# Layer 3's full attention: three PSUM banks for the scores of its first pass, two for the ring of its second

## The chip, the cores and the metric

One core of a Trainium2 chip runs the whole program. The metric is the device time of one execution in microseconds (us): less is better. Five engines work side by side, each on its own queue of instructions in a fixed order: TensorE (PE: matmuls and, apart from them, the loads of their weights, PEld), VectorE (DVE), ScalarE (ACT), GpSimd (POOL) and SyncE (SP, which issues DMAs). They wait for one another through semaphores. Matmuls write to PSUM, which is cut into eight banks of 512 fp32 columns on 128 partitions, and VectorE and ScalarE read them from there.

## What is computed

The program is a chain of fourteen sublayers on a tensor x of 4 sequences of 512 tokens of 128 features: four "layers", each a half-weighted block, an attention and the half-weighted block again. The change concerns layer 3's attention alone, on the sum of everything before it:

```
q = (x @ Wq.T + bq).reshape(b, l, H, HD).transpose(0, 2, 1, 3)      # H = 16 heads of HD = 8
k, v = the same with Wk, bk and Wv, bv
q, k = _apply_rope(q, cos, sin), _apply_rope(k, cos, sin)
scores = jnp.einsum('bhsd,bhed->bhse', q, k) / np.sqrt(HD)          # every token with every token: 512 x 512
attn = jax.nn.softmax(scores, axis=-1)
out = jnp.einsum('bhse,bhed->bhsd', attn, v)
x = x + out.transpose(0, 2, 1, 3).reshape(b, l, e) @ Wo.T + bo
```

No mask is applied, so each of the 16 heads of each of the 4 sequences has a full 512 x 512 table of scores. On either side of it stand the two halves of layer 3's other block (`l3_layer`), which is local attention over windows of 64 tokens and a gated feed-forward.

## The kernel before

**Slots.** The program is a list of units, one for each sublayer and sequence, and slot k does three things side by side: the core of unit k, the preparation ("pre") of unit k + 1 and the closing work ("post") of unit k - 1. The steps of these streams are merged on every engine in an order that is written out by hand for each slot (`ORDERS`, strings such as `a4b1c2`: four steps of stream a, one of b, two of c). An engine goes from one slot to the next without a barrier. The change keeps all of these strings as they are, so every engine's instructions keep their order. Full attention has four slots, one for each sequence; below they are called passes 0 to 3. Pre and post work that runs beside the core is called side work here. In pass 0 it is the post of a layer-3 block (L663, L388, the gated feed-forward at L2502 to L2536) and the pre of the next attention (L388, L439, the turns at L586 with their copies at L595); in passes 1 and 2 the post of the attention before (L688, L715, L720) and again the pre of the next; in pass 3 the pre of a layer-3 block (L2199, L2206, L2242 to L2304).

**The core of the attention, `attend8`.** It serves three kinds of attention (FULL, CAUSAL, BLOCK32). It works through the heads in four groups of four and computes every score twice.

- First pass: `score(i)`, L1151, i = 0 to 63, multiplies one tile of 128 queries with all 512 keys into a bank of `SCORES`. VectorE takes the negated row maximum of it (L1251). With NS banks, score i may start only when the maximum of score i - NS is done (the wait in `score`).
- GpSimd splits a group's maxima into three bf16 parts and writes them beside the queries (L1261, L1267), TensorE turns the queries with them (`turn_q`, L1170, two pairs for each group) and ScalarE copies them back (L1277).
- Second pass: `shifted_score(i)`, L1187, i = 0 to 63, computes the scores transposed, keys by queries, with the maximum already subtracted, into a bank of the ring `RING`; ScalarE takes the exponential of it (L1300) into one of eight buffers. The turned queries of `turn_q` go through the same ring. With NR banks, entry n of the ring may be written only when ScalarE is done with entry n - NR.
- `weigh`, L1210: after every four shifted scores, eight instructions multiply the probabilities of four heads and one tile of keys with the values into the bank `OUT`; ScalarE copies the result of a group (L1283). It weighs what was issued at least three units before.

In TensorE's order the first `LEAD` = 22 first-pass scores stand alone, with side work between them. Then come a turn and, for i = 0 to 41, a shifted score and a first-pass score by turns (score 22 + i beside shifted score i); for i = 42 to 63 there are only shifted scores. Four units and a `weigh` are called a quad below, quads 0 to 15. `half_rows` gives even and odd heads different halves of the array's rows, so two neighbouring matmuls of either pass can run at the same time if nothing holds the second one.

**Banks.** Of the eight, attend8 has six (`SCORES`, `RING` and `OUT`); 6 and 7 are those of the pre and of the post work.

Of the kernel before, what the change touches and what calls it, by code (L numbers as in the profile page):

```python
# [1065 lines left out]
FULL, CAUSAL, BLOCK32 = range(3)  # L1066


def attend8(nc, m, note, a, kind, before):
# [23 lines left out]
    weighed = [max(r for r, unit in enumerate(second) if unit[0][1] in kts or kind == BLOCK32) for kts in kinds]  # L1093
    NW = len(weighed)
    LEAD = N1 + 6
    SCORES, RING, OUT = (0, 1), (2, 3, 4), 5
    NS, NR = len(SCORES), len(RING)
    TURN_AT = max(N2 - 3, 0)
    PROBS = 8
# [460 lines left out]
def l1_ffn_core(nc, m, note, a, b, l, before):  # L1560
    return attend8(nc, m, note, a, CAUSAL, before)
# [544 lines left out]
def l2_attn_core(nc, m, note, a, b, l, before):  # L2106
    return attend8(nc, m, note, a, BLOCK32, before)
# [16 lines left out]
def l3_attn_core(nc, m, note, a, b, l, before):  # L2124
    return attend8(nc, m, note, a, FULL, before)
# [1318 lines left out]
```

## Times and profile before

| | us |
|---|---|
| median of 3 runs | 2942.89 |
| lowest and highest | 2940.99, 2950.08 |
| the profiled execution | 2941.67 |
| its span, first to last instruction | 2939.9 |
| TensorE, VectorE, ScalarE busy over the span | 2544.9, 2167.9, 1664.1 |
| from the first score of pass 0 to the last weighing of pass 3 | 323.6 |

The page of the profile gives busy time and the costliest groups over the whole span; the four passes of full attention are 11% of it, so they are read from windows. "PEclk" there is the clock that TensorE was granted, as a share of 2.4 GHz; 0.5 is 1.2 GHz. A busy TensorE is not TensorE at its peak: the time of a matmul includes the drain of its pipeline.

### The profile page before, as it was taken

How to read it: one execution, taken by the hardware profiler on the slowest of the kernel's cores; microseconds unless marked ns; L12 is line 12 of the kernel's file. 1: busy time of each engine (PE TensorE's matmuls, PEld its weight loads, DVE VectorE, ACT ScalarE, POOL GpSimd, SP SyncE). 2: the span in 40 equal slices, each digit the busy share in tenths (PEclk: the TensorE clock that was granted, in tenths of full speed). 3: DMA queues.
4: the chain of work that ended last, by engine and by line, in shares of the span. 5: the costliest groups of instructions: out<-in, count | busy, mean ns of one | idle time of the engine just before them, and what ended most of it. 6: DMA issues, size and time to landing. Idle time of an engine off the chain costs nothing.

```text
span 2939.9 us, 63499 instructions
## 1 busy us (share of the span) xinstructions
PE 2544.9 (87%) x24589; PEld 1617.3 (55%) x24589; DVE 2167.9 (74%) x5133; ACT 1664.1 (57%) x4036; POOL 787.8 (27%) x810
## 2 busy tenths in 40 slices
PE   6878889788898888988877988999988889989998
PEld 3556666554455544547755875565653222556655
DVE  4856557778887668877567567888877777888883
ACT  2334443466642367753476546767747666676773
POOL 1010001111111111121332246546511114455650
PEclk9879998899999999999999999999989998999999
DMA  3623420000000000014600661010100000001001
GB/s 114 243 41 57 81 62 1 1 1 1 1 1 1 1 1 1 1 58 168 252 6 1 216 217 30 15 28 17 28 3 3 1 1 13 16 16 28 18 19 28
DMA packets 123078, 131.95 MB, mean 45 GB/s; under 512 B 81941, under 2 KB 101653, under 8 KB 121242
## 3 DMA queue, kind: packets, MB, share of 16 engines
q1 hardware_dynamic: 120250, 122.70, 14.0%
q8 instruction: 196, 3.21, 0.5%
q0 software_dynamic: 2048, 4.20, 0.4%
q10 hardware_dynamic: 480, 0.98, 0.1%
q14 instruction: 104, 0.85, 0.1%
HBM read 80.73 MB, written 29.04 MB: 37 GB/s over the span
## 4 chain that ended last, share of the span: by engine, by line
PE 45%; DVE 27%; ACT 10%; issue 7%; POOL 5%; DMA 2%; SPq 0%; DVEq 0%; POOLq 0%; ACTq 0%
DVE nm L1251 6%; PE ps L1210 4%; PE ps L586 3%; PE ps L1990 3%; PE ps L1187 3%; PE ps L2199 3%; PE ps L1151 3%; PE ps L2365 2%; ACT hand L550 2%; PE ps L663 2%; PE ps L439 2%; DVE pre L2285 2%; PE ps L2502 2%; POOL ss L2276 1%; PE ps L265 1%
## 5 line engine op out<-in xcount | busy, mean ns | idle before, releaser
L1251 DVE TENSOR_REDUCE nm<-ps 128x2 f32<-128x256 f32 (+2 forms) x704 | 424.0, 636 | 65.3 <-PE ps L1151 42.4
L1300 ACT ACTIVATE core<-ps 128x512 f32<-128x512 f32 x672 | 358.7, 591 | 93.0 <-PE ps L1192 48.4
L380 POOL TENSOR_TENSOR rstd<-ve,weights 128x4 f32<-128x4 f32 x80 | 83.0, 1038 | 879.5 <-DVE ve L357 828.1
L2271 POOL TENSOR_TENSOR pre<-pre,sin 128x512 f32<-128x512 f32 x128 | 231.2, 1825 | 226.9 <-ACT pre L2242 200.1
L1151 PE MATMUL ps<-hand 128*128 128x128 bf16 (+4 forms) x1024 | 246.0, 314 | 44.9 <-DVE nm L1251 39.8
L550 ACT COPY hand<-ps 64x512 bf16<-64x512 bf16 x336 | 194.7, 579 | 132.1 <-PE ps L586 81.7
L1187 PE MATMUL ps<-hand 128*128 128x128 bf16 (+4 forms) x1024 | 225.3, 307 | 21.7 <-ACT hand L550 15.1
L2405 ACT ACTIVATE core<-ps,nm 128x128 f32<-128x128 f32 x512 | 181.9, 379 | 67.0 <-DVE nm L2422 66.0
L2276 POOL TENSOR_TENSOR ss<-ss,weights 128x16 f32<-128x16 f32 x64 | 196.6, 3072 | 71.6 <-DVE ss L2291 69.9
L2199 PE MATMUL ps<-weights,pre 128*128 128x512 f32 x384 | 200.0, 624 | 11.2 <-ACT hand L2253 6.6
L1261 POOL CAST hand<-nm 128x16 bf16<-128x16 f32 x192 | 59.0, 308 | 492.6 <-DVE nm L1251 484.3
L1210 PE MATMUL ps<-core,hand 128*32 128x512 f32 (+3 forms) x2048 | 179.4, 445 | 8.3 <-ACT otok L1283 5.6
L265 PE MATMUL ps<-identb 128*128 128x256 bf16 x1052 | 165.6, 286 | 16.9 <-PEq L3046 14.3
L1187 PEld LDWEIGHTS ps<-hand 128*128 128x128 bf16 (+1 forms) x1024 | 81.6, 98 | 179.1 <-ACT core L1300 94.9
L1151 PEld LDWEIGHTS ps<-hand 128*128 128x128 bf16 (+1 forms) x1024 | 86.1, 98 | 162.9 <-DVE nm L1251 112.4
L2365 PE MATMUL ps<-hand 64*64 64x128 f32 (+1 forms) x2048 | 136.2, 273 | 0.0
L2365 PEld LDWEIGHTS ps<-hand 64*64 64x64 f32 x2048 | 104.7, 135 | 44.4 <-issue 44.4
L265 PEld LDWEIGHTS ps<-identb 128*128 128x128 bf16 x1052 | 100.3, 102 | 50.5 <-issue 35.1
L586 PE MATMUL ps<-identb,hand 128*128 128x128 bf16 x768 | 79.4, 229 | 55.4 <-DVE pre L502 17.4
L2502 PE MATMUL ps<-post,weights 128*128 128x512 f32 (+1 forms) x192 | 105.6, 632 | 22.3 <-DVE post L2530 13.8
L2422 DVE TENSOR_REDUCE nm<-ps 128x4 f32<-128x512 f32 x128 | 87.2, 682 | 44.3 <-PE ps L2365 43.9
L2285 DVE TENSOR_TENSOR pre<-pre,cos 128x1024 f32<-128x1024 f32 x64 | 108.0, 1688 | 13.9 <-ACT pre L2242 13.8
(352 smaller groups left out, 6313.6 us busy)
## 6 DMA issues: line engine op xcount, KB each, us to landing
hand<-in_experts SPq DMA_DIRECT2D x48, 836.0 KB, 4.7
shear<-post SPq DMA_DIRECT2D x64, 256.0 KB
core<-in_experts SPq DMA_DIRECT2D x12, 836.0 KB, 5.1
core<-shear SPq DMA_DIRECT2D x128, 64.0 KB, 2.2
hand<-hand SPq DMA_DIRECT2D x16, 512.0 KB, 4.4
hand<-hand SPq DMA_DIRECT2D x16, 384.0 KB, 5.6
core<-in_stream SPq DMA_DIRECT2D x2, 2048.0 KB, 7.7
shear<-pre SPq DMA_DIRECT2D x16, 256.0 KB
```

What stands on the lines that cost most here:

```text
L265: nc.tensor.matmul(out, m.identb, m.identb.unsqueeze(1).to_broadcast([P, FILL // P, P]), start=True, stop=True)
L550: ins = copy(a.QX[64 * e:64 * e + 64, q_slot(2 * pair + e), :], src[64 * e:64 * e + 64, :])
L1151: ins = nc.tensor.matmul(b[:, n * nk:(n + 1) * nk], q[:, qt * P:(qt + 1) * P], k[:, lo:lo + nk], start=kind != BLOCK32 and n == 0, stop=Tr ...
L1187: ins = nc.tensor.matmul(b[:, n * w:(n + 1) * w], k[:, kt * P:(kt + 1) * P], q[:, s:z], start=kind != BLOCK32 and n == 0, stop=True, skip_ ...
L1210: ins = nc.tensor.matmul(m.ps[32 * j:32 * j + 32, OUT, s:z], a.V[:, kt, 9 * h:9 * h + 32], prob8[:, i % PROBS, n * w:(n + 1) * w], start=( ...
L1251: nc.vector.tensor_reduce(nm_of(unit), src, AX.X, ALU.max, negate=True).then_inc(negmax, 1)
L1300: nc.scalar.activation(prob8[:, i % PROBS, 0:w], m.ps[:, RING[at % NR], 0:w], ACT.Exp).then_inc(ring_out, 1)
L2199: nc.tensor.matmul(banks[at % N], s.hT[:, t * P:(t + 1) * P], qkv[:, l, i, :], start=True, stop=True).then_inc(lane.filled, 1)
L2271: ins = nc.gpsimd.tensor_tensor(o[:, :, :, z:z + hl], x[:, :, :, y0:y0 + hl], sn[:, t, :, z:z + hl].unsqueeze(2).to_broadcast([P, 2, LH, h ...
L2276: nc.gpsimd.tensor_tensor(m.ss[:, 1, 0:2 * LH], m.ss[:, 0, 0:2 * LH], m.weight["half"][:, 0:2 * LH], ALU.pow).then_inc(rooted, 1)
L2365: ins = nc.tensor.matmul(out[rows, r * P + at:(r + 1) * P], a.Q3[rows, c, n * WIN:(n + 1) * WIN], a.K3[rows, c, lo:(n + 1) * WIN], start=F ...
L2405: nc.scalar.activation(prob[:, i % NP3, r * P:(r + 1) * P], bank(m, S[i % 2])[:, r * P:(r + 1) * P], ACT.Exp, bias=m.nm[:, 4 * i + r:4 * i ...
```

## The change

One line. For full attention the six banks are dealt out anew; the two other kinds keep theirs. Nothing else of the program changes, and no instruction is added, removed or moved.

```diff
     LEAD = N1 + 6
-    SCORES, RING, OUT = (0, 1), (2, 3, 4), 5
+    SCORES, RING, OUT = ((0, 1, 2), (3, 4), 5) if kind == FULL else ((0, 1), (2, 3, 4), 5)
     NS, NR = len(SCORES), len(RING)
```

NS becomes 3: score i waits for the maximum of score i - 3, not i - 2. NR becomes 2: a ring entry waits until ScalarE is done with the entry two before it, not three.

## Rows read from the trace of the kernel before

**Rows 1.** Instruction groups of the four passes: count, busy, mean ns, idle before and releaser.

```profile
L1251 DVE TENSOR_REDUCE nm<-ps 128x1 f32<-128x512 f32 x256 | 164.2, 684 | 36.6 <-PE ps L1151 34.0
L1300 ACT ACTIVATE core<-ps 128x512 f32<-128x512 f32 x256 | 140.4, 614 | 30.4 <-PE ps L1187 29.8
L1151 PE MATMUL ps<-hand 64*128 64x512 bf16 x256 | 88.4, 424 | 25.0 <-DVE nm L1251 23.6 <-ACT core L1300 0.4
L1187 PE MATMUL ps<-hand 64*128 64x512 bf16 x256 | 72.1, 391 | 3.1 <-ACT core L1300 2.0 <-ACT hand L1277 0.5
```

**Rows 2.** Busy time by stretch: stretch, length, each engine, clock, DMA share, GB/s.

```profile
2202.90:2247.10 44.20, 40.24 (x236) 12.14 (x235) 38.59 (x75) 37.66 (x76) 8.66 (x17) 1.00 0.02 4
...
2267.10:2287.20 20.10, 16.14 (x52) 5.31 (x49) 14.51 (x24) 3.50 (x11) 1.25 (x5) 0.66 0.00 1
2287.20:2325.10 37.90, 33.46 (x224) 11.01 (x224) 35.51 (x64) 29.55 (x60) 6.10 (x14) 1.00 0.00 1
2325.10:2343.10 18.00, 16.22 (x128) 5.84 (x126) 6.09 (x19) 15.07 (x28) 2.27 (x6) 1.00 0.00 1
...
2362.10:2400.30 38.20, 32.97 (x225) 10.70 (x225) 35.04 (x60) 30.06 (x60) 6.00 (x13) 1.00 0.00 1
...
2439.60:2480.20 40.60, 39.54 (x220) 13.05 (x219) 36.98 (x60) 32.75 (x64) 17.72 (x17) 1.00 0.00 1
```

**Rows 3.** Timeline, first 22 scores of pass 1: start, length, instruction, [idle before].

```profile
2271.32 0.58 PE L1151 MATMUL ps<-hand 64*128 64x512 bf16 x1 [0.21 <-DVE nm L1251]
...
2271.83 1.12 PE L388 MATMUL ps<-weights,pre 128*128 128x128 f32 x4
...
2276.20 1.65 PE L439 MATMUL ps<-weights,pre 128*128 128x384 f32 x2
```

**Rows 4.** The same stretch, VectorE's maxima.

```profile
2267.58 5.05 DVE L1251 TENSOR_REDUCE nm<-ps 128x1 f32<-128x512 f32 x8 [1.85 <-PE ps L1151]
...
2273.53 3.48 DVE L1251 TENSOR_REDUCE nm<-ps 128x1 f32<-128x512 f32 x5 [0.89 <-PE ps L1151]
...
2278.75 3.48 DVE L1251 TENSOR_REDUCE nm<-ps 128x1 f32<-128x512 f32 x5 [1.74 <-PE ps L1151]
...
2283.97 1.29 DVE L1251 TENSOR_REDUCE nm<-ps 128x1 f32<-128x512 f32 x2 [1.74 <-PE ps L1151]
```

**Rows 5.** Timeline, quad 5 of pass 1, which has both passes' scores.

```profile
2307.60 0.39 PE L1187 MATMUL ps<-hand 64*128 64x512 bf16 x2
...
2308.02 2.06 ACT L1300 ACTIVATE core<-ps 128x512 f32<-128x512 f32 x4 [0.26 <-PE ps L1187]
...
2309.67 0.37 PE L1151 MATMUL ps<-hand 64*128 64x512 bf16 x1 [0.30 <-DVE nm L1251]
```

**Rows 6.** Timeline, quad 14 of pass 1, which has shifted scores alone.

```profile
2338.64 0.60 PE L1187 MATMUL ps<-hand 64*128 64x512 bf16 x3
...
2339.07 2.06 ACT L1300 ACTIVATE core<-ps 128x512 f32<-128x512 f32 x4 [0.32 <-PE ps L1187]
...
2339.72 0.39 PE L1187 MATMUL ps<-hand 64*128 64x512 bf16 x1 [0.47 <-ACT core L1300]
...
2340.03 1.07 PE L1210 MATMUL ps<-core,hand 128*32 128x512 f32 x8
```

**Rows 7.** Timeline, quads 12 and 13 of pass 1.

```profile
2334.27 1.03 ACT L595 COPY hand<-ps 128x1024 bf16<-128x1024 bf16 x1
...
2334.51 0.39 PE L1187 MATMUL ps<-hand 64*128 64x512 bf16 x2
...
2335.17 2.59 ACT L1300 ACTIVATE core<-ps 128x512 f32<-128x512 f32 x5
...
2335.86 0.88 PE L1187 MATMUL ps<-hand 64*128 64x512 bf16 x2
```

**Rows 8.** Timeline, ScalarE in quad 8 of pass 0.

```profile
2240.84 1.28 ACT L1300 ACT_TABLE_LOAD   x1
2242.13 1.08 ACT L1300 ACTIVATE core<-ps 128x512 f32<-128x512 f32 x2
```

**Rows 9.** The same quad, TensorE.

```profile
2240.26 0.40 PE L1187 MATMUL ps<-hand 64*128 64x512 bf16 x2
...
2242.79 0.39 PE L1187 MATMUL ps<-hand 64*128 64x512 bf16 x1 [0.38 <-ACT core L1300]
```

## Prediction, made before the changed kernel ran

> **What bounds the kernel now.** I read the groups of the four passes first, then the busy times by stretch, then timelines. The groups show the case for the change: before first-pass scores TensorE stood idle 23.6 us for VectorE's maxima, before shifted scores 2.0 us for ScalarE's exponentials [rows 1]. That is 25.6 us of 323.6, and it is the wrong sum to build on, since an idle time says nothing of what would come next. The stretches show three regimes in each pass [rows 2], for which pass 1 stands: a **lead** of 20.1 us (the first 22 scores; ScalarE busy 3.50, the clock at 0.66), a **middle** of 37.9 us (both kinds of scores; VectorE busy 35.51, 94%) and a **tail** of 18.0 us (shifted scores alone; VectorE busy 6.09, TensorE 16.22, ScalarE 15.07). The third score bank can act in the lead and the middle. The third ring bank is used in the middle and the tail. So gain and loss lie in different places and each is costed there.
>
> **The lead.** A lone score and its maximum hold a bank for about 0.39 + 0.68 us plus two handovers. In the lead the first eight maxima take 5.05 us, later ones 3.48 us for five, that is 0.70 each, where TensorE runs at the low clock (a matmul of 0.58 and more) and two banks can't keep VectorE fed [rows 3, 4]. With three banks VectorE's own pace holds, (5.05 - 0.68)/7 = 0.62 us. Some 14 of the 22 scores go by 0.70, so 14 x 0.08 = 1.1 us. The larger part is side work: while TensorE does L388, or L439 and what follows it, VectorE runs dry and waits 0.89, 1.74 and 1.74 us [rows 3, 4]. A third bank lets TensorE begin each block one maximum earlier, 0.62 to 0.70 us, and each wait shrinks by that: 3 x 0.65 = 2.0. The 1.85 us before the first maximum remain: no score existed. Together 3.1 us; laid out score by score with these durations (block at L388 from 2271.83 to about 2270.94, L439 from 2276.20 to 2274.3, the turn about 3.0 us earlier) it is 3.0. The order of GpSimd, which splits the maxima of 16 scores ahead of the turn, doesn't move, and it has 3 us to spare in pass 1. The other leads have the same three or so blocks, some shorter; I take 2.7 us on average: **-11 us** for four, between -7 (pauses only, passes 2 and 3 weaker) and -14.
>
> **The middle.** Upper bound of the gain: VectorE's idle time in the four middles, 5.6 + 2.4 + 3.2 + 3.6 = 14.8 us (length less busy) [rows 2]. It won't all come, for the ring holds the same queue. In quad 5 two shifted scores start at 2307.60, the exponentials at 2308.02 with a pitch of (2.06 - 0.60)/3 = 0.49, and the last first-pass score at 2309.67 [rows 5]. With two ring banks the third shifted score waits for the first exponential, 2308.02 + 0.60 + 0.06 = 2308.68, the fourth for the second, 2309.17, and the last first-pass score, no longer waiting for a maximum, starts 0.22 later, at 2309.39: 0.28 us earlier than now. ScalarE is the faster of the two readers (0.49 against 0.60), so where it has nothing else to do the trade is a small gain; but VectorE can't follow in a middle where it has 6% to spare. I take -1.2 us in passes 1 and 2 each and nothing in pass 3. Where ScalarE has other work in its order, the price is the other way: in quad 8 of pass 0 a table load holds the exponentials until 2242.13, and the second of the two shifted scores of 2240.26 would have to wait for the first of them, 2242.13 + 0.60 + 0.06 = 2242.79, instead of running at once [rows 8, 9]. Queued behind it on TensorE are a score, two side blocks (1.6 us) and the shifted score that now waits for the same exponential until 2242.79; so of the 2.5 us about 2 are lost. Less common, smaller cases are in the same pass. Pass 0: +2. **Middle: 0 us**, between -14 (all of VectorE's idle time) and +8 (2 us of such stalls in every pass).
>
> **The tail.** Here nothing is gained: no first-pass scores are left, and the three-deep ring is what hides ScalarE. Quad 14: three shifted scores start at 2338.64 together, the fourth at 2339.72 when the first exponential is done, the weighing at 2340.03 [rows 6]. With two, the third starts at 2339.07 + 0.60 + 0.05 = 2339.72, the fourth one exponential later, 2340.21, the weighing at 2340.53: +0.49 us, on TensorE, which has no other idle time there to give. ScalarE's own work moves by only 0.1, since its queue was full; but TensorE weighs (1.0 us) between the quads in any case, and the ring is too shallow to hide that. Quads 11 and 14 cost 0.49 each; a block of side work between the pairs (0.55 us of turns) doesn't help, as the fourth waits for the second exponential still. Quads 12 and 13 hold copies of ScalarE's: the second shifted score of 2334.51 must wait for the exponential that starts at 2335.17, after the copy of 1.03 us, that is until 2335.83, +1.3; the next ones, which now wait themselves (0.88 us for two), give back 0.4, and quad 13 adds its 0.49: +1.44 for both [rows 7]. Quad 10 has a turn whose entries fill both banks: +0.5 to +0.9; quad 9 +0.2. Pass 1: 0.2 + 0.9 + 0.49 + 1.44 + 0.49 = 3.5. The same count is 3.6 in pass 0, 3.7 in pass 2, and about 4 in pass 3, where a clock of 0.5 in part of the tail stretches it. **Tail: +15 us**, between +8 (0.49 in four quads of each pass and nothing else) and +20.
>
> **Sum.** -11 + 0 + 15 = +4 us. The profiled execution took 2941.67 us (its span is 2939.9, 1.8 us lie around it) and is 1.2 us below the median of the three runs. From the median: 2942.9 + 4 = 2947; from the profiled one 2945.7. I forecast **2946 us**.
>
> **The rivals.**
> *The third score bank wins.* TensorE leaves each middle early and VectorE's idle time goes: -12 in the leads, -12 in the middles, +13 in the tails: -11, so 2932 us. For it speaks that VectorE's reductions are the slower reader (684 against 614 ns, x256 each) and that 34.0 us of its idle time are put down to L1151 [rows 1]. Against it: some 7 us of these are waits for the first score of a pass, four like the 1.85 us of pass 1 [rows 4], and in the middle the waits of the ring sit in the same order.
> *The short ring starves TensorE behind ScalarE's other work* (the case on the other side). The place is every shifted score whose predecessor but one stands behind a copy or a table load on ScalarE; the price is that instruction's length, 1.03 or 1.28 us, once per occurrence, with side work queued behind it [rows 7, 8]. It decides as soon as such stalls aren't covered by VectorE's backlog in the middle: 2 us in each middle (+8) and 20 in the tails, less 11: +17, 2960 us. For it: ScalarE is busy 37.66 of 44.20 us in pass 0's middle [rows 2]. Against: in passes 1 and 2 VectorE is behind then, and hides them.
> *The clock.* The lead shows what spaced-out scores do: TensorE was paced by the maxima, one score every 0.60 us, and its clock fell to 0.66 on average, 1.2 GHz for two thirds of the stretch, while the tail ran at 1.00 [rows 2, 4]. If the tail, with half a microsecond more idle in each quad, falls too for a third of its 16.2 us of work, this third takes twice as long: +5 less the waits it covers, about +3 a pass, +12 on top: 2958 us. The Trainium skill ("TensorE: Matmul & The Clock Gate", A second HAM failure mode: psum-queue depth-cycling) speaks against this change: a TensorE that cycles through a queue of PSUM banks with short idles between groups can lose and regain its full clock over and over. By that rule the time would be this rival's; the trace doesn't bear it out so far, as quad 14, with 0.47 us idle in 2.39, ran at full clock.
> *It does nothing that can be seen*, the bank indices being a relabelling where neither wait binds: 2943 us. The waits of [rows 1] speak against it.
>
> **How the numbers follow.** The forecast's case has 0.50, the third bank's 0.20, the starved ring's 0.18, the clock's 0.08, no effect 0.04. A measurement of this kernel can tell about 0.3%, 8.8 us, from no change: 2934.1 to 2951.7. The forecast's own range is 2937 to 2955 (lead and tail each off by 4, the middle by 5), so 0.06 of its 0.50 are slower than that bound. Faster: 0.20. Same: 0.44 + 0.04 and a little of the two slow cases, 0.50. Slower: 0.30. The range of 8 in 10 reaches into both sides: 2931 to 2961.
>
> **What would show it.** Right: the stretch of the first 22 scores of pass 1 shrinks from 20.1 to about 17 us, its pauses before maxima from 1.74 to about 1.1; the idle time before L1151 put down to L1251 falls from 23.6 to under 14; that before L1187 put down to L1300 grows from 2.0 to 12 or more; quad 14 becomes 2.9 us long; tails of 18.0 become 21.5; the middles keep their length within a microsecond or two. Wrong: leads that shrink by less than 1.5 us, because something other than a bank holds TensorE there; tails that stay near 18 us; middles that shrink by more than 2 us each; a granted clock below 0.9 in the tails of passes 0 to 2. Everything outside the four passes should keep its length; if it doesn't, the sum misses a term.

## The result

The changed kernel takes 2959.61 us (median of seven executions; 2956.06 to 2963.8), the kernel before 2942.7 (2938.76 to 2950.08): 1.0058 times as long, with a 95% interval of 1.0044 to 1.0071, or 16.9 us slower. Forecast were 2946 us, 3 us slower; the range of 2931 to 2961 holds the result by 1.4 us at its upper end, and the narrower range of the forecast's own case, 2937 to 2955, does not hold it.

Where it went is read from the lengths of the three regimes, in each pass: the lead from the first first-pass score to the first shifted score, the middle from there to the start of the weighing that ends quad 9, the tail from there to the next pass (in pass 3 to where the weights of the last weighing are loaded, 0.9 us before its last matmul ends). Summed over the four passes, in us, from one profiled execution each (quad 9, whose 0.2 us a pass the forecast counted with the tail, lies in the middle here):

| | leads | middles | tails | all |
|---|---|---|---|---|
| before | 81.7 | 160.9 | 80.1 | 322.8 |
| changed | 71.4 | 171.2 | 94.7 | 337.3 |
| difference | -10.3 | +10.3 | +14.6 | +14.5 |
| forecast | -11 | 0 | +15 | +4 |

The profiled execution of the changed kernel took 2962.08 us, its span 2960.3, which is 20.4 more than before. Of that 14.5 lie in the passes and 6.3 ahead of them, where the two kernels are alike: pass 0 begins at 2188.08 and not at 2181.78. In the profiles of this study it begins between 2179.5 and 2188.1, and in the changed kernel with only the gelu behind that point altered at 2181.24, so this part is taken as the spread of an execution and no effect.

First the groups of the four passes of the changed kernel, which answer to [rows 1] (count, busy, mean ns, idle before and releaser):

```profile
L1251 DVE TENSOR_REDUCE nm<-ps 128x1 f32<-128x512 f32 x256 | 163.3, 682 | 37.6 <-PE ps L1151 37.1
L1300 ACT ACTIVATE core<-ps 128x512 f32<-128x512 f32 x256 | 143.4, 601 | 46.2 <-PE ps L1187 45.5
L1151 PE MATMUL ps<-hand 64*128 64x512 bf16 x256 | 82.8, 415 | 8.5 <-DVE nm L1251 8.4
L1187 PE MATMUL ps<-hand 64*128 64x512 bf16 x256 | 79.5, 394 | 27.3 <-ACT core L1300 19.3 <-ACT hand L1277 6.1
```

TensorE's idle time ahead of first-pass scores fell from 25.0 to 8.5 us, that ahead of shifted scores rose from 3.1 to 27.3: 16.5 us gone, 24.2 new. Of the 27.3, 6.1 end with L1277, the copy of turned queries, which had 0.5. Both readers stand idle longer than before (VectorE 37.6 against 36.6, ScalarE 46.2 against 30.4), though one of them has a bank more.

The stretches that answer to [rows 2], of the changed kernel (length, busy time of each engine, clock, DMA share, GB/s):

```profile
2206.20:2254.60 48.40, 42.64 (x238) 12.16 (x237) 39.09 (x76) 38.66 (x76) 8.67 (x17) 0.96 0.02 4
...
2277.20:2295.40 18.20, 15.91 (x51) 5.67 (x47) 13.97 (x24) 3.45 (x10) 1.26 (x5) 0.62 0.00 0
2295.40:2334.80 39.40, 33.07 (x229) 10.23 (x232) 35.93 (x64) 30.21 (x60) 6.12 (x14) 1.00 0.00 1
2334.80:2355.90 21.10, 16.90 (x129) 5.83 (x129) 5.90 (x18) 15.73 (x28) 2.27 (x6) 1.00 0.00 1
...
2373.70:2412.00 38.30, 33.33 (x225) 10.42 (x225) 35.20 (x60) 30.44 (x60) 5.92 (x13) 1.00 0.00 1
2412.00:2435.00 23.00, 16.93 (x118) 5.17 (x117) 5.82 (x19) 15.69 (x28) 2.27 (x6) 0.93 0.00 1
...
2452.40:2497.50 45.10, 40.92 (x224) 11.88 (x223) 38.35 (x61) 34.35 (x65) 18.04 (x17) 1.00 0.00 1
2497.50:2525.40 27.90, 21.44 (x109) 6.68 (x112) 11.62 (x26) 17.35 (x33) 10.31 (x9) 0.82 0.15 34
```

Middles: 44.2 became 48.4 (pass 0), 37.9 became 39.4, 38.2 became 38.3 and 40.6 became 45.1 (pass 3). Pass 1 stands for lead and tail: 20.1 became 18.2, 18.0 became 21.1. Next the maxima in the lead of pass 1, against [rows 4]:

```profile
2277.74 4.87 DVE L1251 TENSOR_REDUCE nm<-ps 128x1 f32<-128x512 f32 x8 [2.58 <-PE ps L1151]
2282.89 3.08 DVE L1251 TENSOR_REDUCE nm<-ps 128x1 f32<-128x512 f32 x5 [0.28 <-PE ps L1151]
2287.30 3.08 DVE L1251 TENSOR_REDUCE nm<-ps 128x1 f32<-128x512 f32 x5 [1.34 <-PE ps L1151]
2291.73 1.29 DVE L1251 TENSOR_REDUCE nm<-ps 128x1 f32<-128x512 f32 x2 [1.34 <-PE ps L1151]
```

Pauses of 0.89, 1.74 and 1.74 us became 0.28, 1.34 and 1.34, and five maxima take 3.08 and not 3.48 us, though the granted clock was no higher (0.62 in this lead, 0.66 before). Both parts of the forecast gain are there; the pauses gave 1.4 us of the 2.0 laid out, the pace 1.0 of 1.1, and 0.4 of that is lost again between the last maximum shown and the first shifted score.

Two quads of pass 1, TensorE's timeline in the changed kernel. First quad 5, against [rows 5], with its weighing at the end:

```profile
2316.24 0.39 PE L1187 MATMUL ps<-hand 64*128 64x512 bf16 x2
2316.47 0.38 PE L1151 MATMUL ps<-hand 64*128 64x512 bf16 x2
2317.32 0.39 PE L1187 MATMUL ps<-hand 64*128 64x512 bf16 x1 [0.47 <-ACT core L1300]
2317.55 0.38 PE L1151 MATMUL ps<-hand 64*128 64x512 bf16 x1
2317.81 0.39 PE L1187 MATMUL ps<-hand 64*128 64x512 bf16 x1
2318.03 0.38 PE L1151 MATMUL ps<-hand 64*128 64x512 bf16 x1
2318.34 0.64 PE L1210 MATMUL ps<-core,hand 128*32 128x512 f32 x4
```

Then quad 14, against [rows 6]:

```profile
2350.94 0.39 PE L1187 MATMUL ps<-hand 64*128 64x512 bf16 x2
2352.01 0.87 PE L1187 MATMUL ps<-hand 64*128 64x512 bf16 x2 [0.69 <-ACT core L1300]
2352.82 0.64 PE L1210 MATMUL ps<-core,hand 128*32 128x512 f32 x4
```

In quad 5 the third shifted score waits for the first exponential, the fourth comes 0.49 later, and nothing waits for a maximum: the last first-pass score starts 1.79 us after the first shifted one (2.07 before), and the quad, weighing to weighing, takes 3.09 us, not 3.38. In quad 14 two shifted scores start together where three did, and the quad takes 2.88 us, not 2.39. Both were laid out so in the prediction.

### The profile page after: what moved, and what is told of

The parts are those of the page before. It is cut to its first block, busy times and chain, and to the rows that moved or that the text cites. A ratio compares the mean times of both kernels' runs of the same rounds, so it can differ in the third digit from the quotient of the medians.

```text
span 2960.3 us, 63433 instructions
## 1 busy us (share of the span) xinstructions
PE 2549.8 (86%) x24519; PEld 1620.7 (55%) x24589; DVE 2167.6 (73%) x5133; ACT 1671.4 (56%) x4036; POOL 788.0 (27%) x810
## 4 chain that ended last, share of the span: by engine, by line
PE 45%; DVE 26%; ACT 10%; issue 7%; POOL 5%; DMA 2%; SPq 0%; another core or an unknown queue 0%; DVEq 0%; ACTq 0%; POOLq 0%
DVE nm L1251 5%; PE ps L1210 4%; PE ps L1187 3%; PE ps L586 3%; PE ps L1990 3%; PE ps L2199 3%; PE ps L2365 2%; PE ps L1151 2%; ACT hand L550 2%; PE ps L663 2%; PE ps L439 2%; PE ps L2502 2%; DVE y L1603 2%; DVE pre L2285 2%; POOL ss L2276 1%
## 5 line engine op out<-in xcount | busy, mean ns | idle before, releaser
L1187 PE MATMUL ps<-hand 128*128 128x128 bf16 (+4 forms) x1005 | 226.9, 308 | 42.8 <-ACT core L1300 22.3
L1151 PE MATMUL ps<-hand 128*128 128x128 bf16 (+4 forms) x997 | 232.1, 311 | 27.7 <-DVE nm L1251 24.3
L2276 POOL TENSOR_TENSOR ss<-ss,weights 128x16 f32<-128x16 f32 x64 | 196.7, 3074 | 71.9 <-DVE ss L2291 70.3
L265 PE MATMUL ps<-identb 128*128 128x256 bf16 x1052 | 164.3, 285 | 16.9 <-PEq L3046 14.2
L2365 PEld LDWEIGHTS ps<-hand 64*64 64x64 f32 x2048 | 104.1, 135 | 44.2 <-issue 44.2
```

Source lines behind the costliest of these rows:

```text
L265: nc.tensor.matmul(out, m.identb, m.identb.unsqueeze(1).to_broadcast([P, FILL // P, P]), start=True, stop=True)
L1151: ins = nc.tensor.matmul(b[:, n * nk:(n + 1) * nk], q[:, qt * P:(qt + 1) * P], k[:, lo:lo + nk], start=kind != BLOCK32 and n == 0, stop=Tr ...
L1187: ins = nc.tensor.matmul(b[:, n * w:(n + 1) * w], k[:, kt * P:(kt + 1) * P], q[:, s:z], start=kind != BLOCK32 and n == 0, stop=True, skip_ ...
L2276: nc.gpsimd.tensor_tensor(m.ss[:, 1, 0:2 * LH], m.ss[:, 0, 0:2 * LH], m.weight["half"][:, 0:2 * LH], ALU.pow).then_inc(rooted, 1)
L2365: ins = nc.tensor.matmul(out[rows, r * P + at:(r + 1) * P], a.Q3[rows, c, n * WIN:(n + 1) * WIN], a.K3[rows, c, lo:(n + 1) * WIN], start=F ...
```

## Experiments

Two theories were set against each other for the 10.3 us of the middles, which the forecast did not have. A: the ring of two costs there what it costs in the tail, above all where the turned queries fill it and where ScalarE has other work in front of an exponential. B: the third score bank lets TensorE run into side work that waits for VectorE. The other runs test lead and tail apart, and look for a deal of the banks that keeps the gain alone. For those where banks change with the phase, the round robin was replaced by a plan: for each score or ring entry, in TensorE's order, the bank of those allowed that was used longest ago, and a wait for that bank's last user.

**The short ring alone.**

```diff
-    SCORES, RING, OUT = (0, 1), (2, 3, 4), 5
+    SCORES, RING, OUT = ((0, 1), (2, 3), 5) if kind == FULL else ((0, 1), (2, 3, 4), 5)
```

> Full attention keeps two score banks and has a ring of two (one PSUM bank stands unused), so only the loss of the change is in it. Theory A (the short ring costs in the middle too: turned queries that fill both its entries, and shifted scores behind other work of ScalarE): leads unchanged within 0.5 us each, tails +3.7 us on average as in the changed kernel (+15), middles +10 or more over the four passes, since the third score bank isn't there to give anything back: 25 to 35 us slower than before. Theory B (the middle loses because TensorE, with three score banks, runs ahead into side work that waits for VectorE, and the ring has no part in it): middles +0 to +3, tails +15: 15 to 18 us slower.

Measured: 2968.83 us against 2940.7, ratio 1.0096 (1.0076 to 1.0116), 28 us slower. Leads 80.8, middles 173.9, tails 97.4: -0.9, +13.0 and +17.3. So the middles lose as much without the third score bank as with it, and a little more; theory B as the only cause falls. On balance the third score bank, which the changed kernel has beside the short ring, gives 2.7 us back in the middles. The tails are 2.7 us longer than in the changed kernel. The low clock has a part in that: the tail of pass 3 had a granted clock of 0.71 here, 0.82 in the changed kernel.

**The third score bank in the leads alone.** The first 22 scores go over banks 0, 1 and 2, then everything as before.

```diff
+    LEAD_SCORES, SCORES, RING, TAIL_RING, OUT = (((0, 1, 2), (0, 1), (2, 3, 4), (2, 3, 4), 5) if kind == FULL else ...
```

> Only the first 22 scores of each pass go over three banks (the third is a bank of the ring, which is empty then); from the first turn on two and three as before. If the four leads give what they gave in the changed kernel (-3.0, -2.0, -1.3, -4.1 us) and nothing is given back: 10 us faster than before, middles and tails unchanged within 1 us each. If VectorE's work only moves (it is the bound of the middles of passes 1 and 2), up to half comes back in the middles: 5 us faster.

Measured: 2935.59 us against 2940.7, ratio 0.9981 (0.9970 to 0.9992), 5.1 us faster. In its profile leads 70.3, middles 161.1, tails 80.1: -11.4 us in the leads and nothing given back. The profiled execution took 2929.91 us, the median is 5.7 us above it. So the profile shows the gain of the first expectation and the median half of it. The leads themselves move with the granted clock: with the same three banks, that of pass 0 takes 16.7 us here at 0.80 and 18.2 in the changed kernel at 0.62, that of pass 3 takes 19.3 here at 0.65 and 17.3 there at 0.90. How they fall out in the other executions isn't known, and this stays open. Every quad from quad 1 on is as before to within 0.02 us, so the plan of the banks in itself changes nothing.

**The changed kernel with its third ring bank back in the tail.** Score banks (0, 1, 2), ring (3, 4), and (2, 3, 4) once the last first-pass score is issued.

```diff
+    LEAD_SCORES, SCORES, RING, TAIL_RING, OUT = (((0, 1, 2), (0, 1, 2), (3, 4), (2, 3, 4), 5) if kind == FULL else ...
```

> The changed kernel, but once the last first-pass score of a pass is issued the ring has three banks again (the freed score bank joins it). Both theories: the tails return to their lengths before (about -15 us against the changed kernel), leads and middles stay those of the changed kernel: 0 to 2 us slower than before. If the tail's loss were not the ring's depth but what the middle leaves behind, it would stay 10 us slower or more.

Measured: 2944.42 us against 2940.7, ratio 1.0004 (0.9994 to 1.0015): no difference. Leads 70.4, middles 174.3, tails 77.8. The tails are back, 16.9 us below those of the changed kernel, quads 10 to 14 of passes 0 to 2 at the lengths of before to within 0.15 us. The tail's loss is the depth of the ring, and nothing that the middle leaves behind. The middle's loss stands (3.1 us more than in the changed kernel, of which 2.4 are quad 8 of pass 0, 9.00 us long at a granted clock of 0.62).

**Five banks in the leads.** While the ring is empty its three banks take scores.

```diff
+    LEAD_SCORES, SCORES, RING, TAIL_RING, OUT = (((0, 1, 2, 3, 4), (0, 1), (2, 3, 4), (2, 3, 4), 5) if kind == FULL else ...
```

> The first 22 scores go over five banks (all that the core has but the output's), then two and three as before. Pauses before maxima inside the leads (0.89 to 1.78 us before) should vanish, the first one of each pass stays. If VectorE is what a lead is worth: 4 us a pass, 14 to 18 us faster than before. If what comes next (the split of the maxima on GpSimd, then the turn) sets the end of a lead, little more than with three banks: 10 us faster.

Measured: 2928.15 us against 2940.7, ratio 0.9955 (0.9939 to 0.9970), 12.5 us faster. Leads 62.4, middles 168.8, tails 78.5: -19.3, +7.9 and -1.6. The leads give more than expected, but a part comes back in the middles of passes 0 and 3 (45.5 and 46.9, against 44.1 and 40.7). In pass 3 quad 0 grew from 5.09 to 9.82 us and quad 1 from 4.87 to 6.36. TensorE came to this middle early: behind the first shifted score it stood idle 1.27 us for a maximum, which VectorE had behind its side work (L2315, 2.00 us), and then ran at a granted clock of 0.64 in quad 0 and 0.75 in quad 1.

**Turned queries out of the short ring.** As the first experiment, but the turns use the bank that stood unused there, one half of it for each pair, and ScalarE waits for both.

```diff
+                ring_bank[turn_at(g, n)] = (4, None if g == 0 else ("ring", turn_at(g - 1, 1)))
-            act.wait_ge(ring_in, at + 1)
+            act.wait_ge(ring_in, turn_at(g, 1) + 1 if APART else at + 1)
```

> Two score banks and a ring of two, as in the run with the short ring alone, but the turned queries leave the ring: both halves of a turn go into the bank that stood unused, and ScalarE copies them when both are there. If the turns that fill both entries of the ring make the middle's loss: middles fall from 173.9 us over the four passes by 6 to 8 us (the quads with a turn, 2 and 6, lost 6.2 of 10.3 us in the changed kernel), the tails by 2 to 3 us (quad 10): 8 to 11 us faster than the short ring alone, some 18 to 20 slower than before. If the loss of those quads is only the depth of two like elsewhere, or the copies' own time, under 3 us faster.

Measured: 2965.76 us against 2943.03, ratio 1.0083 (1.0066 to 1.0099), where the short ring alone had 1.0096: some 4 us better at most, within the two intervals. Leads 82.2, middles 172.1, tails 86.6. Quads 2, 6 and 10 of the four passes, those with a turn, take 59.7 us before, 66.0 with the short ring and 55.1 with the turns apart. So the edit brings back all that these quads lost, and 4.6 us more, since the turns now take no ring entry at all; it doesn't measure the loss of the turns alone. And of 5.9 us that quads 2 and 6 win, the middles keep 1.8: their neighbours grow (quad 3 of pass 0 from 3.37 to 4.27, quad 7 of pass 3 from 4.04 to 5.08; quad 8 there from 3.58 to 4.73, with the clock at 0.64). Of the 10.8 us in the tails 6.6 are pass 3, which ran at full clock here and at 0.71 there. The expected 6 to 8 us in the middles weren't there, and the tails gave more than the 2 to 3 expected.

**Five banks for the lead, five for the tail.** As with five in the lead; the score banks join the ring after the last first-pass score.

```diff
+    LEAD_SCORES, SCORES, RING, TAIL_RING, OUT = (((0, 1, 2, 3, 4), (0, 1), (2, 3, 4), (0, 1, 2, 3, 4), 5) if kind == FULL else ...
```

> As the run with five banks for the first 22 scores, and when the last first-pass score is issued the ring gets the two score banks as well: two, then three, then five. TensorE's waits for exponentials in quads 9 to 15 (some 1.0 us a pass before) go, but the last exponential of a pass still ends it: tails 0.5 to 1.5 us shorter each, 3 to 5 us faster than with five banks in the lead alone, 2924 us. If TensorE's own work bounds the tails, nothing: 2928 us.

Measured: 2920.58 us against 2943.03, ratio 0.9921 (0.9903 to 0.9939), 22 us faster: the best of all. Leads 60.9, middles 165.0, tails 76.7. The stretches of pass 1 (lead, middle, tail) of this kernel:

```profile
2267.40:2281.60 14.20, 12.69 (x51) 4.42 (x47) 13.33 (x24) 3.45 (x10) 1.26 (x5) 0.76 0.00 1
2281.60:2319.90 38.30, 33.75 (x228) 11.06 (x231) 36.23 (x65) 29.71 (x60) 6.13 (x14) 1.00 0.00 1
2319.90:2337.00 17.10, 15.20 (x130) 5.40 (x130) 5.98 (x19) 14.97 (x28) 2.28 (x6) 1.00 0.00 1
```

The lead is 14.2 us long, with VectorE busy 13.3 of them, and the tail 17.1, 0.9 less than before. Quad 14 takes 2.07 us in every pass. As with five banks in the lead alone, a part comes back in the middles, most of it in quads 0 and 1 of pass 0 (6.06 and 4.90 us against 4.65 and 3.38, at granted clocks of 0.76 and 0.60).

**Without the gelu.** ScalarE's gelu of layer 3's feed-forward (L2523) becomes the identity, in the changed kernel and in the kernel before; this part of the computation is left out.

```diff
-            nc.scalar.activation(s.gel[0:size[c], c, :], s.gel[0:size[c], c, :], ACT.Gelu).then_inc(gelus, 1)
+            nc.scalar.activation(s.gel[0:size[c], c, :], s.gel[0:size[c], c, :], ACT.Identity).then_inc(gelus, 1)
```

> The changed kernel with the gelu of layer 3's feed-forward left out (the identity in its place), so that ScalarE loads no table between exponentials in the middle of pass 0; the same edit of the kernel before runs beside it. If other work of ScalarE in front of an exponential makes quad 8 of pass 0 1.4 us longer in the changed kernel, the two kernels without the gelu differ there by less than 0.5 us, and the whole middle of pass 0 by 2 to 3 us instead of 4.2. If the table load has no part in it, the quad's difference stays above 1 us.

> The kernel before with the same edit: the gelu of layer 3's feed-forward left out. It is the partner of the changed kernel without the gelu and has no claim of its own: the middle of pass 0 gets shorter by the table loads or VectorE's work takes their place.

Measured, one execution each: 2958.6 us and 2938.05 us. Quad 8 of pass 0 takes 6.18 us in the changed kernel and 6.20 in the kernel before, where with the gelu it was 6.56 and 5.15. The difference is gone, but not in the way that was meant: it is the kernel before that got longer, and both had a granted clock of 0.72 in this quad. So the pair doesn't tell what the table load costs. Quads 4, 5 and 6, which have no table load in either, differ as they did (4.55 against 3.70, 5.22 against 4.56, 6.85 against 6.01 us).

## Why the prediction was right, and where it wasn't

**The lead** was right in both its parts, the pace of the maxima and the shorter pauses, and in size in the profiled execution (-10.3 for -11). In pass 1 alone 3.0 us were laid out and 1.9 came; passes 0 and 3 gave more (-3.0 and -4.1). Some of that agreement is luck. The lead of pass 3 had a granted clock of 0.90, against 0.68 before; with the same three banks at 0.65 it saved 2.1 us (second experiment), so 2 us of the 4.1 go with the clock. Whether three banks raise the clock there isn't shown. In the median the same leads alone were worth 5.1 us.

**The tail** was right (+14.6 for +15), and where the clock stayed full quad by quad: quads 11 and 14 +0.49 as worked out (in passes 0 and 1 both), quads 12 and 13 of pass 1 from 5.75 to 7.17, +1.42 for +1.44, quad 10 there +0.80 for +0.9. The third experiment takes it back by one bank. The sum is closer than its parts: the tail of pass 0 grew by 2.7 us and not 3.4 (quad 9 left out), and that of pass 2 by 5.1 and not 3.5, of which 1.3 are a low clock in quad 13.

**The middle** is the step that failed: 0 was forecast, +10.3 came, or about +8.5 without quad 9 (+1.7, of which 0.8 had been put into the tail), either way beyond the upper end of +8 that the text gave it. That the total lies in the range is owed to the width of the range and not to this term. Three things were wrong in it.

First, the turns. Their price was put into the tail (quad 10) and forgotten in the middle, where quads 2 and 6 of each pass have one too. These eight quads grew from 36.9 to 43.0 us, +6.2. That is what they lost by themselves, not what the turns cost the middles: with the turns out of the short ring the middles gained only 1.8 us. Quad 2 of pass 1 in the changed kernel, TensorE:

```profile
2303.92 0.39 PE L1187 MATMUL ps<-hand 64*128 64x512 bf16 x2
2304.15 0.38 PE L1151 MATMUL ps<-hand 64*128 64x512 bf16 x2
2305.36 0.66 PE L688 MATMUL ps<-weights,otok 128*128 128x128 f32 x4 [0.83 <-DVE post L699]
2305.85 0.61 PE L1170 MATMUL ps<-identb,hand 128*128 128x128 bf16 x8
2306.91 0.39 PE L1187 MATMUL ps<-hand 64*128 64x512 bf16 x1 [0.46 <-ACT hand L1277]
```

and in the kernel before:

```profile
2296.28 0.39 PE L1187 MATMUL ps<-hand 64*128 64x512 bf16 x2
2296.51 0.57 PE L1151 MATMUL ps<-hand 64*128 64x512 bf16 x2
2297.18 0.66 PE L688 MATMUL ps<-weights,otok 128*128 128x128 f32 x4
2297.67 0.61 PE L1170 MATMUL ps<-identb,hand 128*128 128x128 bf16 x8
2298.21 0.39 PE L1187 MATMUL ps<-hand 64*128 64x512 bf16 x1
```

The shifted score behind the turn now waits for the turn's first copy (0.46 us idle), since the two pairs fill the ring. Above it is theory B after all, as a smaller part: TensorE reaches the side block L688 early and waits 0.83 us for L699, which VectorE has in its order behind maxima. With the short ring and two score banks this quad takes 4.47 us, with three score banks 5.01, before 4.01; so here half of the loss is the ring's and half comes with the third score bank. The neighbours pay part of it back (quads 1 and 3: 3.09 and 3.73, from 3.50 and 4.01).

Second, the stalls behind ScalarE's other work were counted as a rare event of pass 0 (+2; +4.2 came) and as nothing in pass 3 (+4.5 came). The +2 was above all the price of the table load in quad 8 of pass 0, some 2 us, and there the changed kernel shows:

```profile
2245.15 1.93 PE L1210 MATMUL ps<-core,hand 128*32 128x512 f32 x8
2247.02 0.40 PE L1187 MATMUL ps<-hand 64*128 64x512 bf16 x1
...
2248.09 0.39 PE L1187 MATMUL ps<-hand 64*128 64x512 bf16 x1 [0.46 <-ACT core L1300]
```

The second shifted score does wait for the exponential behind the load, but only 0.46 us, and from the first shifted score to the next weighing the quad takes 4.69 us, not 4.15: +0.54. The other 0.87 of its +1.41 us is the weighing at its start, at the low clock (1.93 us, 1.07 before). Quad 7 (+0.6) is a matter of the clock too: with the same ring at full clock it took 5.87 us (third experiment), before 5.93. What the prediction called less common, smaller cases weighed more: quads 4 and 5 of pass 0, both at full clock, lost 0.85 and 0.65. In quad 5 it is ScalarE's L397, which waits for the block L388 of TensorE:

```profile
2228.34 0.78 ACT L397 ACTIVATE post<-ps,weights 128x512 f32<-128x512 f32 x1 [1.87 <-PE ps L388]
2229.02 1.66 ACT L1300 ACTIVATE core<-ps 128x512 f32<-128x512 f32 x3
...
2229.66 0.39 PE L1187 MATMUL ps<-hand 64*128 64x512 bf16 x1 [0.91 <-ACT core L1300]
```

Quad 1 of pass 3 shows what was overlooked, TensorE first:

```profile
2460.36 0.39 PE L1187 MATMUL ps<-hand 64*128 64x512 bf16 x1
...
2461.17 0.39 PE L1187 MATMUL ps<-hand 64*128 64x512 bf16 x1 [0.21 <-ACT core L1300]
...
2461.70 0.66 PE L2206 MATMUL ps<-weights,pre 128*128 128x128 f32 x4
...
2463.54 0.39 PE L1187 MATMUL ps<-hand 64*128 64x512 bf16 x1 [0.64 <-ACT core L1300]
```

then ScalarE:

```profile
2460.03 0.59 ACT L2237 COPY hand<-ps 128x512 f32<-128x512 f32 x1 [1.50 <-PE ps L2199]
2460.51 1.09 ACT L1300 ACTIVATE core<-ps 128x512 f32<-128x512 f32 x2
2462.40 0.59 ACT L2253 COPY hand<-ps 128x512 f32<-128x512 f32 x1 [0.80 <-PE ps L2206]
2462.88 1.68 ACT L1300 ACTIVATE core<-ps 128x512 f32<-128x512 f32 x3
```

A shifted score waits for an exponential, the side block L2206 is queued behind it on TensorE, ScalarE's copy of that block (L2253) has to come before the next exponential in ScalarE's order and idles 0.80 us for it, and the last shifted score waits for that exponential. The ring's wait goes round twice between the two engines; the quad grew from 4.87 to 6.20 us. In the kernel before L2253 waited for nothing. The prediction priced such a wait once, at the length of one instruction. The same 1.33 us are in every kernel with a ring of two in the middle (the changed one and four others, 6.20 us each). With a ring of three the quad takes 4.87 us, in the kernel before with and without the gelu, with three banks in the lead, and with five in lead and tail; five in the lead alone is the exception (6.36, at a granted clock of 0.75).

Third, VectorE's backlog was taken for cover. In pass 1 it was 94% busy in the middle and is 91% busy now, with the same work (35.51 and 35.93 us): a wait of TensorE's that starts a maximum late can hardly be caught up by an engine with 6% to spare. This third point is read from the busy times; no run tests it alone. The gain of 1.2 us in passes 1 and 2 was +1.4 and +0.2.

**The rivals.** The case that came nearest is the one where the short ring starves TensorE behind ScalarE: its place, its condition and its 2960 us are what was measured, with 10.3 us in the middles for the 8 and 14.6 in the tails for the 20 given there. It had 0.18. Its price of one instruction's length for each stall was not. The third bank's victory is refuted: it had -12 in the middles, where +10.3 came. The clock's rival is there in small. The changed kernel had a low stretch in the middle of pass 0 (0.96) and in the tail of pass 2 (0.93), where before both ran at 1.00, and its last tail had 0.82. In pass 2 its quad 13 took 4.75 us, 3.43 in three other kernels with a ring of two in the tail that ran it at full clock. There the rule of the Trainium skill ("TensorE: Matmul & The Clock Gate", A second HAM failure mode: psum-queue depth-cycling) points the right way, with 1.3 us in this quad; the tails of passes 0 and 1 kept the full clock with the same waits, so it is no more than a share of the 14.6 us. Over all the profiles it is hardly chance: of the twelve tails of passes 0 to 2 in the four kernels with a ring of two there, five have a stretch below full clock, of the eighteen in the six kernels with three or five banks none. In quads 7 and 8 of pass 0 all five kernels with a ring of two in the middle have one, and two of the five with three. So by these counts the short ring seems to cost through the clock too, in some passes and some executions. In the changed kernel 1.3 us of the tails and 1.5 of the middle of pass 0 are seen to be that; what it costs in the median isn't known, with one profile of each kernel.

## What to carry to other kernels

When a bank moves from one queue to another, walk each kind of stretch by itself: here the idle times asked for the third score bank over the whole stage (23.6 us against 2.0), but it gained 10.3 us in the leads and some 2.7 in the middles, and in the leads the ring's banks stood empty anyway. Dealing the banks by phase, the idle ring's to the scores in the lead and the idle scores' to the ring in the tail, took 22 us off where the fixed deal put 17 on. And a wait for an engine that holds other work in a fixed order is priced by the round trips through that order, with everything that periodically goes through the same ring counted in, not by one instruction.

## What the runs showed of the hardware

Quads repeat to 0.01 us from kernel to kernel as long as banks and clock are the same (quad 11 of pass 0 is 2.88 us in all four kernels with a ring of two there, 2.39 in those with three). What moves is where TensorE's clock falls to 1.2 GHz: quad 8 of pass 0, with the middle's banks of before, took 5.15, 5.58 and 6.20 us at granted clocks of 1.00, 0.81 and 0.72 (the kernel before, five banks in the lead, and the kernel before without the gelu). Before the low stretch of the changed kernel there TensorE had stood idle for 1.58 us, for VectorE's L502. Also, five banks in the lead brought VectorE's work of a lead (13.3 us busy of 14.2 in pass 1) near its own pace of 0.60 us a maximum.
